# Attention on one core: a longer lead, transposes two steps apart, the loop written out, and value products in pairs

## The reference

```python
attn_scores = jnp.einsum('bihd,bjhd->bhij', q, k) / scale
li = x @ rel_W[:, :d].T
lj = x @ rel_W[:, d:].T
logits = li[:, :, None, :] + lj[:, None, :, :] + rel_b
relation_probs = jax.nn.softmax(logits, axis=-1)
bias = jnp.einsum('bijk,hk->bhij', relation_probs, logical_bias)
gate = jax.nn.sigmoid(x @ gate_W.T + gate_b)
gate = jnp.transpose(gate, (0, 2, 1))[..., None]
attn_scores = attn_scores + gate * bias
attn_weights = jax.nn.softmax(attn_scores, axis=-1)
out = jnp.einsum('bhij,bjhd->bihd', attn_weights, v).reshape(b, s, d)
return out @ Wo.T + bo
```

## Time and profile before

| | us |
|---|---|
| median of 3 runs | 3916.91 |
| lowest and highest | 3913.67, 3921.83 |
| profiled execution, its own time | 3901.86 |
| its span | 3900.1 |
| busy in the span: TensorE matmuls | 3160.8 (81%) |
| VectorE | 2553.7 (65%) |
| ScalarE | 2071.3 (53%) |
| GpSimd | 2291.9 (59%) |
| mean granted TensorE clock (1 is full) | 0.928 |

### The profile page before, as it was taken

One profiled execution on the slowest core, in us unless ns is written; L12 is line 12 of the kernel. 1 busy time (PEld: TensorE's weight loads), 2 busy tenths in 40 slices (PEclk: granted clock), 3 DMA queues, 4 the chain that ended last, 5 costly groups with the idle time before them and its releaser, 6 DMA issues. The chain is left out here.

```text
span 3900.1 us, 130011 instructions
## 1 busy us (share of the span) xinstructions
PE 3160.8 (81%) x52983; PEld 2315.4 (59%) x52983; DVE 2553.7 (65%) x3404; ACT 2071.3 (53%) x2481; POOL 2291.9 (59%) x1606
## 2 busy tenths in 40 slices
PE   3169988898988899768888888888888888888885
PEld 2157766676766677535566565656565566556564
DVE  5367776676767676356667666666666666666664
ACT  2135554454545454435566665656665665566563
POOL 1334444454444443167777777777777777777773
PEclk7579999999999999989999999999999999999997
DMA  4344444444444444132212212312232222221221
GB/s 103 63 69 76 81 71 76 80 75 71 81 76 72 76 81 71 56 95 51 58 49 71 70 48 50 92 48 49 60 80 50 55 73 61 52 56 48 50 59 36
DMA packets 277292, 257.58 MB, mean 66 GB/s; under 512 B 106263, under 2 KB 220840, under 8 KB 276824
## 3 DMA queue, kind: packets, MB, share of 16 engines
q1 hardware_dynamic: 276232, 252.24, 30.5%
q10 hardware_dynamic: 720, 0.20, 0.0%
HBM read 98.30 MB, written 40.37 MB: 36 GB/s over the span
## 5 line engine op out<-in xcount | busy, mean ns | idle before, releaser
L659 ACT ACTIVATE prob<-psS 128x1024 f32<-128x1024 f32 x512 | 524.7, 1025 | 700.0 <-PE psS L536 699.2
L810 DVE TENSOR_TENSOR colmax<-psS,colmax 128x1024 f32<-128x1024 f32 x480 | 585.3, 1219 | 426.0 <-PE psS L536 423.7
L536 PE MATMUL psS<-diag,pst 128*128 128x64 bf16 x16384 | 595.4, 196 | 15.8 <-issue 15.7
L536 PEld LDWEIGHTS psS<-diag,pst 128*128 128x128 f16 x16384 | 529.0, 100 | 76.7 <-issue 24.9
L528 PE MATMUL psS<-qst,kst 48*128 48x128 bf16 (+1 forms) x8192 | 386.3, 223 | 217.1 <-DMA pst<-p_parts 136.9
L1268 PE MATMUL R<-wqkv,xsT 128*128 (+1 forms) x1152 | 555.4, 605 | 1.5 <-ACT qT L1404 1.1
L528 PEld LDWEIGHTS psS<-qst,kst 48*128 48x128 bf16 (+1 forms) x8192 | 240.8, 96 | 376.8 <-issue 209.7
L1534 POOL TENSOR_TENSOR pr<-pr,rnq 128x1024 f32<-128x1024 f32 x96 | 182.7, 1903 | 465.4 <-DVE pr L1616 465.4
L508 POOL TENSOR_TENSOR rel<-f,top 128x1024 f32<-128x1024 f32 x61 | 144.5, 2369 | 512.3 <-DVE top L815 511.8
L570 PE MATMUL psO<-prob,v 128*9 128x128 f32 x8192 | 329.4, 279 | 3.3 <-issue 2.7
L1268 PEld LDWEIGHTS R<-wqkv,xsT 128*128 128x128 f32 x1152 | 197.5, 191 | 162.2 <-issue 160.6
(11 more groups left out here) (190 smaller groups left out, 6488.5 us busy)
## 6 DMA issues: line engine op xcount, KB each, us to landing
v<-vs SPq DMA_DIRECT2D x576, 128.0 KB, 2.4
pst<-p_parts SPq DMA_DIRECT2D x512, 128.0 KB, 4.9
p_parts<-stage SPq DMA_DIRECT2D x64, 512.0 KB, 3.0
v<-vs SPq DMA_DIRECT2D x384, 64.0 KB, 2.0
wqkv<-in_L_ffn_Wqkv SPq DMA_DIRECT2D x18, 512.0 KB
q_stack<-qpart SPq DMA_DIRECT2D x6, 512.0 KB
qst<-q_stack SPq DMA_DIRECT2D x32, 96.0 KB, 5.6
wo<-in_L_ffn_Wo SPq DMA_DIRECT2D x6, 512.0 KB
```

Of the source, the lines that this page charges most:

```text
L536: last = pe.matmul(o, pst[:, par, g, P * jb:P * (jb + 1)], diag[:, par, g, h0:h0 + HH // 2, :], start=False, stop=(g == NG - 1), skip_grou ...
L659: act.activation(prob[:, st % 2, :], psS[:, slot_of("b", st)].rearrange("p a b -> p (a b)"), ACT.Exp)\
L810: dve.tensor_tensor(dst, src, dst, ALU.max).then_inc(a_read, 1)
```

## The change

- `LEAD` is 24 instead of 22. The slot of a tile of the lead-in follows from it.
- `max0`, `max1` and `guard` are at steps 8, 10 and 13 instead of 10, 11 and 13, and in the lead-in behind tiles 17, 19 and 22 instead of 17, 18 and 20; VectorE reads them behind tiles 18, 20 and 23.
- The value products of the steps st - 2 and st - 1 both follow the relations of each even step st; odd steps have none. The last two follow the last body.
- `prob` has three buffers by the step's number, and ScalarE waits for the values of three steps before.
- The loop over `body` is written out on all five engines.

```diff
-LEAD = 22
+LEAD = 24
...
-        prob = sb("prob", [P, 2, HH * P])
+        prob = sb("prob", [P, 3, HH * P])
...
-                ev[10], ev[11], ev[13] = "max0", "max1", "guard"
+                ev[8], ev[10], ev[13] = "max0", "max1", "guard"
...
-                return (st + LEAD + 2) % 3
+                return st % 3
...
-                                     prob[:, jb % 2, col:col + P], start=(jb == 0 and s == 0),
+                                     prob[:, b % 3, col:col + P], start=(jb == 0 and s == 0),
...
-                    if not (first and st == 0):
-                        pu, pj = divmod(st - 1, NB)
-                        values(b - 1, pj, pu % 2, it * 4 + pu)
+                    if st % 2 == 0 and b > 0:
+                        for s in (st - 2, st - 1):
+                            pu, pj = divmod(s, NB)
+                            values(b + s - st, pj, pu % 2, it * 4 + pu)
...
-                if a == 18:
+                if a == 19:
                     through_m("max1", 1, -1, -1)
-                if a == 20:
+                if a == 22:
                     through_m("guard", 2, -1, -1)
             body(0, first=True)
-            with pe.Fori(1, 7) as it:
+            for it in range(1, 7):
                 body(it)
             body(7, last=True)
+            values(8 * 4 * NB - 2, NB - 2, 1, 0)
             values(8 * 4 * NB - 1, NB - 1, 1, 0)
...
-                if not (first and st < 2):
-
-                    act.wait_ge(pv_done, b - 1)
-                act.activation(prob[:, st % 2, :], psS[:, slot_of("b", st)].rearrange("p a b -> p (a b)"), ACT.Exp)\
+                if b >= 3:
+
+                    act.wait_ge(pv_done, b - 2)
+                act.activation(prob[:, b % 3, :], psS[:, slot_of("b", st)].rearrange("p a b -> p (a b)"), ACT.Exp)\
...
-                        if a == 19:
+                        if a == 20:
                             read_m("max1", 1, -1, [0])
-                        if a == 21:
+                        if a == 23:
                             read_m("guard", 2, -1, [5])
```

More of the change, by code:

```diff
@@ L710, in _ @@
             body(0, first=True)
-            with act.Fori(1, 7) as it:
+            for it in range(1, 7):
                 body(it)
@@ L795, in _ @@
             body(0, first=True)
-            with pool.Fori(1, 7) as it:
+            for it in range(1, 7):
                 body(it)
@@ L942, in _ @@
             body(0, first=True)
-            with dve.Fori(1, 7) as it:
+            for it in range(1, 7):
                 body(it)
@@ L1032, in _ @@
             body(0, first=True)
-            with sp.Fori(1, 7) as it:
+            for it in range(1, 7):
                 body(it)
```

## The result

The changed kernel takes 3923.4 us (median of 20 runs, 3912.0 to 3979.9) and the kernel before 3914.6 us (20 runs, 3908.3 to 3924.0) on the same chip. The ratio is 1.002, with a 95% interval of 1.001 to 1.0029: 0.2% slower, 8 to 9 us, just at what a measurement of this kernel can tell from no change. One run of the changed kernel, the 3979.9, had a mean granted clock of 0.817, the other 19 (3912.0 to 3934.1 us) had 0.926 to 0.930, and the ratio leaves it out. The forecast was 3927 us.

A forecast was written before the change was run, and what follows sets the result against it. The prediction took VectorE's maximum, through PSUM slot reuse, to set the 2.29 us step. Its terms, -42 + 75 - 58 + 40 - 2 - 8 + 5 = +10 us, gave 3927 us, range 3886 to 3960 for 8 in 10.

The forecast's parts named there:

- Jumps, -42: Attention loop written out: five jumps go, 8.5 us each with the lower clock behind them, -42 us.
- Pairs, +75: Value products of two steps together: a pair of steps costs 4.89 us instead of 4.58, +75 us over 244 pairs.
- -8 for covered stops: TensorE's remaining issue stops, 25 us, are partly covered by an odd step's slack or the new wait: -8 us.
- Transposes, -58: Guard transposes further apart: excess of a unit falls from 5.2 to 3.37 us, -1.85 for 31 units, -58 us.
- Lead, +40 for the wait: Lead of 24 needs the fourth quarter of pst sooner: TensorE waits 2.6 us in each of 15 blocks, +40 us.
- Clock, +5: Step behind a stop of some 3 us costs 0.4 more, 15 times, less lapses with guard stops: +5 us.
- The stops in straight code: TensorE's issue stops outside the jumps, 25 us, stay when the loop is written out.
- the first (the quarter isn't late): Rival: pst's quarter lands 3 us sooner against the steps, +40 and +5 fall away, 3882 us; 0.18 together with half of it.
- the third (the chain meets GpSimd): Rival: VectorE's guard chain still runs while GpSimd works, +50 us, so 3977 us; chance 0.06.
- the second: Rival: TensorE's issue stops in straight code go with the loop, -25 + 8, so 3910 us; chance 0.04.
- the fourth: Rival: a pair's second value group on TensorE costs its upper bound, +30 us, so 3957 us; chance 0.13.
- fifth rival (the parts cancel): Rival: over the whole kernel the parts cancel to within 8 us, 3909 to 3925 us; chance 0.28.

The follow-up runs named there:

- e1_loop_only: The kernel before with only the loop over body written out: 3867.1 us, ratio 0.9897 to the kernel before.
- e3_pairs_only: The kernel before with the loop written out, value products in pairs and three prob buffers; lead 22 and old transposes: 3930.7 us, ratio 1.0064 to the kernel before.
- e6_guards_act: The changed kernel with ScalarE issuing the guard DMAs behind the exponential of step 14, instead of SyncE: 3923.9 us, ratio 1.0016 to the kernel before.
- e4_lead23: The kernel before with the loop written out, lead 23, transposes at 9, 11 and 13, values in every step: 3861.7 us, ratio 0.9851.
- e10_sooner_single: The changed kernel without pairs, reciprocals and ScalarE's conversion sooner, quarter sent ahead of the guards: 3847.4 us, ratio 0.9825 to the kernel before.
- e11_sooner_after: The changed kernel, pairs kept, reciprocals and ScalarE's conversion sooner, quarter sent ahead of the guards: 3852.6 us, ratio 0.9838 to the kernel before.
- e12_total_after_chain: e10_sooner_single with GpSimd's sum held back every second window until VectorE's guard chain has ended: 3821.1 us, ratio 0.9754 to the kernel before.
- e2_no_pairs: The changed kernel with value products one step at a time again: 3863.8 us, ratio 0.9886 to the kernel before.

## Why the prediction was right, point by point

The time was right to 4 us, in part by luck: two terms missed by some 13 us each, with opposite signs, and the cause named for a third was wrong. The terms, by the prediction's own steps:

- **Jumps, -42.** Measured -43 by the medians, -39 in attention.
- **Pairs, +75, with -8 for covered stops.** The steps are the 2.60 and 2.29 predicted (0.99 us for two value groups against the assumed 1.00). The second group takes 0.43 us of the 0.44, and the odd step waits 0.52 us of the 0.65. Measured alone +65, of the predicted 67, but +55 as the last of the four parts. Stops for issue are 20.1 us in the changed kernel and 26.3 in e1_loop_only, so 6 of the 8 us.
- **Transposes, -58.** Steps 8 to 13 of the median unit sum to 17.88 us in e1_loop_only and to 16.99 in the changed kernel, in which the pairs add 3 x 0.31. That is -1.82 a unit; of the predicted -1.85, these steps had 0.59 x 2 + 1.3 less 0.45 + 1.4 + 2.37, or -1.74. The chain step costs 1.17 more than an even step, predicted 1.3, with the chain at 1.8 us and the reciprocal behind it, as forecast. The median flatters it: against e3_pairs_only, which has the pairs and the old places, these steps are 42 us shorter over all 31 units, 1.4 a unit. Step 14 gives another 29 (see the clock, below).
- **Lead, +40 for the wait.** The steps that hold it grew by 41.0 us against e3_pairs_only. The amount was right and the named cause was not. "SP sends it only behind the guards" is true of the kernel before, whose timeline shows the quarter finished at 451.81, 2.6 us before SyncE comes to it:

```profile
449.68 2.13 POOL L750 TENSOR_TENSOR stage<-rel,stage 128x1024 f16<-128x1024 f32 x1 [1.54 <-ACT stage L688]
...
452.50 1.60 SPq L993 DMA_DIRECT2D qst<-guardT  x2
454.37 0.39 SPq L971 DMA_DIRECT2D p_parts<-stage  x1
```

  In the changed kernel it is finished at 462.60 and sent at 463.10. The prediction had seen that the last reciprocal moves behind the chain and that GpSimd waits for it, and used this only to say that the chain meets no GpSimd; it did not follow the same delay on to L752 and the copy. The late quarter came out right by taking SyncE's issue times of before relative to step 0, and those of after are close to the same (2.1 us after tile b in place of 2.2), though something else sets them. That they agree is luck. The error had a price: e6_guards_act was built on it and gained nothing.
- **Clock, +5.** The prediction gave 0.4 us to the step behind each wait. It costs more: relations at 1.89 instead of 1.11, and value groups at 1.90 instead of 1.06, at half the clock. The step behind the wait, with the stops in it, grew by 1.1 us in each of 15 blocks against e3_pairs_only, 17 us in all. Against it the lapses behind the guards' stop at step 14 are gone: 15.8 us of excess there in e1_loop_only, 29.0 in e3_pairs_only. One such step of the latter, 4.59 us in place of 2.60, with the step ahead of it, of which the guards' wait is a part:

```profile
591.90:596.15 4.25, 2.23 (x55) 1.63 (x49) 3.99 (x8) 1.97 (x2) 3.09 (x3) 0.90 0.01 4
596.15:600.74 4.59, 4.59 (x80) 3.55 (x82) 1.41 (x2) 1.02 (x1) 1.38 (x1) 0.50 0.02 4
```

  The two terms were mis-sized with opposite signs. Put together, attention falls by 14.5 us from e3_pairs_only to the changed kernel, and the prediction had -58 + 40 - 2 + 5 = -15 for that. In it steps 3 to 5 add 57.5 us where 45 were forecast, and steps 8 to 14 give 71 where 58 were.
- **The stops in straight code** stay when the loop goes, as said, though not in the same number: 15 before L536 in the earlier trace rows, 14 in e1_loop_only, 11 in the changed kernel. By the Trainium skill ("Runtime: NRT & Kernel Launch", Instruction fetch mechanics) crossing a block of instructions is mostly hidden; e1_loop_only has no jump in attention and still 26.3 us in 27 waits for issue before L528, L536 and L570. That these are fetches was argued from their regular places, and not shown.

Rivals: of the five, the first (the quarter isn't late) and the third (the chain meets GpSimd) did not happen here, nor did the second (20.1 us of stops are left) or the fourth (the second group at its upper bound of 0.56). Forecast and fifth rival (the parts cancel) can't be told apart: 3923.4 lies in the rival's 3909 to 3925, and the difference to the kernel before, 8.7 us, just above its 8. The chain does meet GpSimd in e4_lead23 and in e10_sooner_single. e11_sooner_after is the first rival made true, 3852.6 us, below the 3882 given to it, since it also took the reciprocal out of the chain step.

## What to carry to other kernels

An operation that is moved ahead of others on its engine makes those later: follow each of them to the last queue and landing, not only to the engine that waits next. Measure parts that have opposite signs one by one; here four parts of 39 to 57 us, two up and two down, left 12, and the useful versions lay in undoing one (the pairs) and repairing one (the lead). Work that is grouped on the engine that is nearly the bound makes its steps uneven, and with few buffers to the engine that is the bound, each long step costs and no short one pays it back.

## What the runs showed of the hardware

- **VectorE's small operations wait for GpSimd's running one.** The scaling, the two subtractions and the two copies to bf16 of the chain take 0.17 us alone. The traces of all fourteen kernels hold 479 that started while a GpSimd operation ran. Of these 471 took 0.2 to 1.3 us (three of them 2.04), and every one ended 0.02 to 0.03 us after GpSimd's; the other 8 had started less than 0.2 us ahead of its end. None of the 1761 others was long. The last copy of the chain, from bf16 to f32 (L861 before, L863 in e11_sooner_after), was never held: 54 ran their 0.18 us beside GpSimd. The kernel before has two held ones a unit, as in the earlier trace rows. The maxima (one input in PSUM) and the reciprocals kept their 1.22 and 0.94 us beside GpSimd. The Trainium skill ("SBUF — State Buffer", SBUF: two separate sides) says that a VectorE operation with two SBUF inputs (beside a GpSimd operation that reads SBUF), or in a 2-port mode, and a GpSimd operation exclude each other for a whole instruction. The trace agrees for the subtractions, which have two SBUF inputs, and for the maxima, which have one. e12_total_after_chain turned it into 26 us at the step of the chain.
- **A wait costs twice.** After 3.7 us without work TensorE came back at half its clock for the next tile and its values. A stop of 2.0 us for issue did the same in e10_sooner_single (relations at 1.89 us behind it).
- **Stops for issue move with the timing.** They were 27.4 us in e2_no_pairs, 54.7 in e10_sooner_single and 46.9 in e12_total_after_chain, with the same instructions on TensorE. What decides this stays open.
